# Flamingo gated block: halves of the exponentials added on GpSimd ahead of the ones product

## What is computed

```python
def _mha(query, key, value, Wq, bq, Wk, bk, Wv, bv, Wo, bo):
    q, k, v = ...                      # projections, split into 16 heads of 32
    scores = jnp.einsum('bhqd,bhkd->bhqk', q, k) / jnp.sqrt(jnp.asarray(dk, q.dtype))
    p = jax.nn.softmax(scores, axis=-1)
    x = jnp.einsum('bhqk,bhkd->bhqd', p, v)
    return jnp.einsum('bsd,ed->bse', x.transpose(0, 2, 1, 3).reshape(B, S, D), Wo) + bo
...
x = x + jnp.tanh(g_xattn[0]) * mha(layernorm(x), ctx, ctx, ...)
x = x + jnp.tanh(g_ffn[0]) * ffn(layernorm(x), ...)
```

## Time and profile before

| | before |
|---|---|
| median of 3 runs | 1910.21 us (1909.71 to 1914.14) |
| the profiled execution | 1910.74 us, span 1909.0 us |
| granted TensorE clock, mean | 0.97 of 2.4 GHz |
| TensorE busy | 1687.6 us, 88% |
| VectorE busy | 1441.6 us, 76% |
| ScalarE busy | 866.3 us, 45% |
| GpSimd busy | 497.3 us, 26% |
| attention phase | up to about 1350 us |
| ones product, busy | 135.7 us, 2048 records |
| product with v, busy | 138.1 us, 2048 records |

### The profile page before, as it was taken

The page is one execution under the profiler, slowest core; times in us unless marked ns, Lnnn a source line. Parts: engine busy times, 40 slices in busy tenths (PEclk is TensorE's granted clock), DMA queues, the critical chain, the costliest instruction groups (busy, mean ns, idle before and its releaser), DMA issues.

```text
span 1909.0 us, 36308 instructions
## 1 busy us (share of the span) xinstructions
PE 1687.6 (88%) x12892; PEld 832.0 (44%) x12892; DVE 1441.6 (76%) x1917; ACT 866.3 (45%) x1036; POOL 497.3 (26%) x686
## 2 busy tenths in 40 slices
PE   3788999989999899998999989986599999989787
PEld 3354444544445444454444444433344444434333
DVE  6648788787786877868778687777877778878555
ACT  2243433434335343353443533414777777756242
POOL 6123323223232232322323223212000000006634
PEclk6999999999999999999999999999799999999899
DMA  5233332323323233233332332225235454115897
GB/s 187 67 109 92 88 105 73 110 87 88 109 81 101 87 86 112 84 94 105 84 100 85 91 107 61 78 56 199 94 121 210 165 203 150 45 45 213 337 419 296
DMA packets 132189, 239.73 MB, mean 126 GB/s; under 512 B 17456, under 2 KB 66608, under 8 KB 129584
## 3 DMA queue, kind: packets, MB, share of 16 engines
q1 hardware_dynamic: 132144, 239.14, 38.1%
HBM read 126.10 MB, written 62.39 MB: 99 GB/s over the span
## 4 chain that ended last, share of the span: by engine, by line
issue 38%; PE 31%; DVE 16%; POOL 8%; DMA 5%; ACT 2%; POOLq 0%; DVEq 0%; SPq 0%; ACTq 0%
PE bank L1244 11%; PE bank L1149 5%; PE bank L1151 5%; PE bank L1150 5%; PE spair L1226 4%; DMA x<-out_dram 4%; DVE mx L842 3%; POOL xl L485 3%; DVE rs L834 3%; POOL yh L559 3%; DVE xbuf L806 2%; DVE v L826 1%; ACT xh L580 1%; DVE ndev L866 1%; DVE parts L821 1%
## 5 line engine op out<-in xcount | busy, mean ns | idle before, releaser
L593 ACT ACTIVATE pr<-spair 128x1024 f32<-128x1024 f32 x256 | 259.2, 1020 | 142.1 <-PE spair L1226 142.1
L842 DVE TENSOR_REDUCE mx<-spair 128x4 f32<-128x1024 f32 x256 | 304.4, 1212 | 0.0
L834 DVE RECIPROCAL rs<-bank 128x256 f32<-128x256 f32 x128 | 224.6, 1755 | 56.5 <-PE bank L1244 56.1
L821 DVE SCALAR_TENSOR_TENSOR parts<-bank,bqk,parts 128x512 f16<-128x512 f32 x128 | 94.5, 747 | 132.5 <-ACT parts L586 132.5
L515 POOL TENSOR_TENSOR ol<-o,oh 128x256 f16<-128x256 f32 x128 | 86.5, 675 | 389.7 <-ACT oh L602 380.8
L586 ACT ACTIVATE parts<-bank,bqk 128x512 f16<-128x512 f32 x128 | 88.0, 687 | 219.9 <-PE bank L1151 219.9
L1355 PE MATMUL spair<-xqT,wgT 128*128 128x512 bf16 x704 | 181.9, 381 | 1.2 <-ACT xqT L703 1.2
L1355 PE MATMUL spair<-xqT,wuT 128*128 128x512 bf16 x704 | 181.7, 381 | 0.0
L1244 PE MATMUL bank<-pr,v 128*32 128x256 f32 x2048 | 138.1, 387 | 27.2 <-DVE o L836 27.2
L1226 PE MATMUL spair<-stacks 128*128 128x256 f16 x1024 | 152.5, 275 | 6.5 <-DMA stacks<-mT 6.2
L686 ACT ACTIVATE sil<-spair,gsc 128x512 f32<-128x512 f32 x176 | 118.2, 680 | 74.9 <-PE spair L1355 74.9
(11 more groups left out here) (172 smaller groups left out, 3408.8 us busy)
## 6 DMA issues: line engine op xcount, KB each, us to landing
stacks<-parts SPq DMA_DIRECT2D x768, 64.0 KB, 2.0
x<-out_dram SPq DMA_DIRECT2D x32, 1024.0 KB, 11.0
h_spill<-hb SPq DMA_DIRECT2D x10, 2816.0 KB, 9.2
hb<-h_spill SPq DMA_DIRECT2D x10, 2816.0 KB, 15.6
xbuf<-in_x_dram SPq DMA_DIRECT2D x16, 1024.0 KB, 5.3
cbuf<-in_ctx_dram SPq DMA_DIRECT2D x16, 1024.0 KB, 5.3
xres<-in_x_dram SPq DMA_DIRECT2D x16, 1024.0 KB, 5.2
out_dram<-xres SPq DMA_DIRECT2D x16, 1024.0 KB, 4.3
```

The source lines that it names most:

```text
L593: act.activation(pr[:, u % 4, :, :, :].rearrange("p a b q -> p (a b q)"), spair[u % 2][:, :, :].rearrange("p a q -> p (a q)"), ACT.Exp, sc ...
L821: dve.scalar_tensor_tensor(out=parts[:, c, 2 * w + 1, :], in0=pj[g % 3][:, :], scalar=bqk[:, w, c:c + 1], in1=parts[:, c, 2 * w, :], op0=A ...
L834: dve.reciprocal(rs[:, g % 2, :], obank[:, S:2 * S]).then_inc(recip_done, 1)
L842: dve.tensor_reduce(mx[:, h:h + 2, b, :], spair[u % 2][:, :, :].rearrange("p a (q k) -> p a q k", q=KH), AX_X, ALU.max).then_inc(max_done, 1)
```

## The change

The two key halves of each unit's exponentials are added on GpSimd (`add_halves`, 128 partitions x 512 f32 elements) into a new tensor `ph` with four places, and the ones product runs over `ph` alone: four matmuls per group instead of eight. It comes behind the whole v product and waits for the sums of both units. GpSimd's queue is laid out anew: per group g first adds 2g and 2g + 1, then the low half of group g - 2, then in groups 0 to 3 one tile of the residual and in groups 4 to 6 one Newton step; the last two low halves stand behind the loop. `o32` has four buffers instead of two, and `norm` waits for the high and low halves of group g - 4.

```diff
-        o32 = alloc(p1, "o32", [P, 2, S], F32)
...
+        ph = alloc(p1, "ph", [P, 4, 2, S], F32)
+        o32 = alloc(p1, "o32", [P, 4, S], F32)
...
-            def root(n, which):
+            def root_step(n, which, step):
...
+                if step == 0:
+                    wait(pool, guessed[which], n + 1)
+                else:
+                    wait(pool, newton[which], k + 4 * step)
...
-            def residual(j):
+            def add_halves(j, u):
+
+                wait(pool, exp_done, j * NU + u + 1)
+                wait(pool, pv_mm, j * NGR + u // 2 - 1 + 2)
+                pool.tensor_tensor(ph[:, u % 4, :, :], pr[:, u % 4, :, 0, :], pr[:, u % 4, :, 1, :],
+                                   ALU.add).then_inc(halves_added, 1)
+
+            def residual(j, t):
 
                 wait(pool, res_in, j * 16 + 16)
-                for t in range(NT):
-                    pool.tensor_tensor(xres[:, t, :], xres[:, t, :], tgbo[:, :], ALU.add).then_inc(res_bias, 1)
+                pool.tensor_tensor(xres[:, t, :], xres[:, t, :], tgbo[:, :], ALU.add).then_inc(res_bias, 1)
...
             def body(j, nxt):
-                residual(j)
                 for g in range(NGR):
-                    o_low(j, g)
-                    if g == 3 and nxt is not None:
-                        x_rstds(nxt)
+                    add_halves(j, 2 * g)
+                    add_halves(j, 2 * g + 1)
+                    if g >= 2:
+                        o_low(j, g - 2)
+                    if g < NT:
+                        residual(j, g)
+                    elif g < NT + NEWTON and nxt is not None:
+                        root_step(nxt, 0, g - NT)
+                o_low(j, NGR - 2)
+                o_low(j, NGR - 1)
                 if nxt is not None:
                     low_parts(nxt)
                 x1_rstds(j)
...
             def norm(j, g):
                 wait(dve, pv_mm, j * NGR + g + 1 + 2)
-                if g >= 2:
-                    wait(dve, o_hi, j * NGR + g - 1)
-                    wait(dve, o_lo, j * NGR + g - 1)
+                if g >= 4:
+                    wait(dve, o_hi, j * NGR + g - 3)
+                    wait(dve, o_lo, j * NGR + g - 3)
...
-                for ones in (False, True):
-                    for kh in range(KH):
-                        for a in range(HPC):
-                            h = HPC * c + a
-                            at = S if ones else 0
-                            last = pe.matmul(obank[DK * a:DK * a + DK, at:at + S],
-                                             onesP[:, :] if ones else v[:, 2 * b + kh, DK * h:DK * h + DK],
-                                             pr[:, (2 * g + a // 2) % 4, a % 2, kh, :],
-                                             start=(kh == 0), stop=(kh == KH - 1))
+                for kh in range(KH):
+                    for a in range(HPC):
+                        h = HPC * c + a
+                        pe.matmul(obank[DK * a:DK * a + DK, 0:S], v[:, 2 * b + kh, DK * h:DK * h + DK],
+                                  pr[:, (2 * g + a // 2) % 4, a % 2, kh, :], start=(kh == 0), stop=(kh == KH - 1))
+                wait(pe, halves_added, j * NU + 2 * g + 2)
+                for a in range(HPC):
+                    last = pe.matmul(obank[DK * a:DK * a + DK, S:2 * S], onesP[:, :],
+                                     ph[:, (2 * g + a // 2) % 4, a % 2, :], start=True, stop=True)
                 last.then_inc(pv_mm, 1)
```

More of the change, by code:

```diff
@@ L187, in gated_block_kernel @@
         exp_done = sem("exp_done")
+        halves_added = sem("halves_added")
         pv_mm = sem("pv_mm")
@@ L491, in root @@
                 r0 = rt[:, which, :]
-                wait(pool, guessed[which], n + 1)
                 k = n * (4 * NEWTON - 1)
-                for step in range(NEWTON):
[L495 to L505, removed]
+                if step == 0:
+                    wait(pool, guessed[which], n + 1)
+                else:
+                    wait(pool, newton[which], k + 4 * step)
+                pool.tensor_tensor(a[0], r0, r0, ALU.mult).then_inc(newton[which], 1)
+                wait(pool, newton[which], k + 4 * step + 1)
+                pool.tensor_tensor(a[1], a[0], ve[:, which, :], ALU.mult).then_inc(newton[which], 1)
+                wait(pool, newton[which], k + 4 * step + 2, alone=True)
+                pool.tensor_scalar(a[2], a[1], -0.5, 1.5, ALU.mult, ALU.add).then_inc(newton[which], 1)
+                wait(pool, newton[which], k + 4 * step + 3)
+                if step < NEWTON - 1:
+                    pool.tensor_tensor(r0, r0, a[2], ALU.mult).then_inc(newton[which], 1)
+                else:
+                    pool.tensor_tensor(dst[:, :], r0, a[2], ALU.mult).then_inc(done, 1)
+            def root(n, which):
+                for step in range(NEWTON):
+                    root_step(n, which, step)
             def x_rstds(n):
@@ L514, in o_low @@
                 wait(pool, v_mm, j * NT + NT)
-                pool.tensor_tensor(ol[:, c, b * S:b * S + S], o32[:, g % 2, :], oh[:, c, b * S:b * S + S],
+                pool.tensor_tensor(ol[:, c, b * S:b * S + S], o32[:, g % 4, :], oh[:, c, b * S:b * S + S],
                                    ALU.subtract).then_inc(o_lo, 1)
-            def residual(j):
+            def add_halves(j, u):
[4 more added lines that the diff above has]
+            def residual(j, t):
                 wait(pool, res_in, j * 16 + 16)
-                for t in range(NT):
-                    pool.tensor_tensor(xres[:, t, :], xres[:, t, :], tgbo[:, :], ALU.add).then_inc(res_bias, 1)
+                pool.tensor_tensor(xres[:, t, :], xres[:, t, :], tgbo[:, :], ALU.add).then_inc(res_bias, 1)
             def x1_rstds(j):
@@ L601, in o_high @@
                 wait(act, v_mm, j * NT + NT)
-                act.activation(oh[:, c, b * S:b * S + S], o32[:, g % 2, :], ACT.Copy).then_inc(o_hi, 1)
+                act.activation(oh[:, c, b * S:b * S + S], o32[:, g % 4, :], ACT.Copy).then_inc(o_hi, 1)
             def turn_copies(n, ks):
@@ L830, in norm @@
                 wait(dve, pv_mm, j * NGR + g + 1 + 2)
-                if g >= 2:
-                    wait(dve, o_hi, j * NGR + g - 1)
-                    wait(dve, o_lo, j * NGR + g - 1)
+                if g >= 4:
+                    wait(dve, o_hi, j * NGR + g - 3)
+                    wait(dve, o_lo, j * NGR + g - 3)
                 dve.reciprocal(rs[:, g % 2, :], obank[:, S:2 * S]).then_inc(recip_done, 1)
                 wait(dve, recip_done, j * NGR + g + 1)
-                dve.tensor_tensor(o32[:, g % 2, :], obank[:, 0:S], rs[:, g % 2, :], ALU.mult).then_inc(norm_done, 1)
+                dve.tensor_tensor(o32[:, g % 4, :], obank[:, 0:S], rs[:, g % 2, :], ALU.mult).then_inc(norm_done, 1)
             def key_max(i, u):
```

## The result

The changed kernel takes 1964.08 us (median of 4 runs, 1961.82 to 1966.43) against 1911.76 of the kernel before in the same comparison: 1.0278 times as long, 95% interval 1.0265 to 1.0291. The profiled execution has a span of 1961.8 us, 52.9 above the 1909.0 of before.

A forecast was written before the change was run, and what follows sets the result against it. TensorE bounds pairs 2 to 6, VectorE the body's head and tail. Inner body 4.14 - 2.15 + 0.5 + 0.2 = +2.7 us, thirteen +35; with other bodies +39 on 1910.7 gives 1950, range 1915 to 1968.

The forecast's parts named there:

- rival (c): GpSimd's adds are dearer, 1.4 us each rather than 1.24: +13, 1963 us; chance 0.13.
- turns with ndev: At a body's head, adds 0 and 1 alternate with VectorE's four ndev spread instructions: +1.9 us.
- root stall: Pair 5's ones product waits 0.5 us because a root step stands ahead of adds 10 and 11 on GpSimd.
- new waits, met: TensorE's added wait between v and ones of each pair, already satisfied: 0.2 us a body (0 to 0.75).
- part 1: Pairs 1 to 6 each drop 8 of 16 ones records, 0.43 us: at most 2.6 us a body, 36 over 14.
- Parts 2 and 3: GpSimd adds take 1.24 us each; adds 2 and 3 wait behind xres's load, delaying pair 1's next score 2.24 us.
- Part 4: At a body's head, adds 0 and 1 take turns with VectorE's ndev spread: +1.9 us, pair 1's next score +4.14.
- rival (a): VectorE keeps its turn through the four ndev instructions, so only the load's wait holds: +11, 1921 us; chance 0.22.
- Part 5: Root steps in pairs 4 to 6: the first, awaiting VectorE's guess, delays adds 10 and 11; pair 5 stalls 0.5 us.
- Part 6: New wait between v and ones costs 0.2 us a body (0 to 0.75); four o32 buffers and later low halves 0.
- The other bodies: Outside the thirteen inner bodies: first -2.5 us, fourteenth +2.2 (no root), last +4.5 (2 to 5).

The follow-up runs named there:

- experiment 4: Changed kernel with residual tile t moved to group t + 1, so adds 2 and 3 stand ahead of the xres load wait: 1938.65 us, ratio 1.015.
- experiment 7: Changed kernel, pair 0's ones from both halves (no adds 0/1), residual tiles one group later; root steps in groups 5-7: 1884.74 us, in groups 4-6: 1880.62 us.
- experiment 6: Changed kernel with unread filler matmuls in pair 1, ten ahead of v and eight ahead of ones, all waits kept: 1939.5 us, ratio 1.0146.
- experiment 3: Changed kernel with adds made but TensorE's 16 ones records as before and not waiting for the sums; only later exponentials wait: 1954.73 us, ratio 1.0229.
- experiment 5: Changed kernel with pair 0's ones product from both key halves again and adds 0 and 1 gone: 1926.84 us, ratio 1.0098.

## Why the prediction was right, and where it was short

Forecast was 1950 with 1915 to 1968 and a slower kernel; it took 1964. The sign and the places were right, the size fell short: +52 measured, +39 forecast. The number alone would also fit rival (c), dearer adds, at 1963; but two adds start 1.23 us apart, not 1.4, so it isn't (c). Point by point for an inner body (mean over 13):

| step | forecast, us | measured, us |
|---|---|---|
| v of pair 1 later, turns with ndev | +1.9 | +1.92 |
| ones of pair 1 waits longer for its sums | +2.67 | +2.44 |
| from ones of pair 1 to v of pair 2 | -0.43 | +1.57 |
| v of pair 2 to v of pair 5 | -1.29 | -1.29 |
| v of pair 5 to v of pair 6, root stall in it | +0.1 | -0.06 |
| pair 6 to the next body | -0.43 | -0.56 |
| new waits, met | +0.2 | 0 |
| sum | +2.7 | +4.0 |

- What bounds the kernel: right. Halving the ones product alone gave 2.72 us a body against the 2.6 of part 1; the 0.12 more lie behind pair 6, where part 1 took all that pair 7 gains as swallowed.
- Parts 2 and 3: right. An add's median is 1.27 us, 1.23 from start to start; the load let GpSimd start 9.2 us behind the root (526.23 less 517.04; 9.5 was forecast), and moving the residual removed the wait. Where it was removed, however, the next wait took its place, as experiment 4 shows.
- Part 4: right, the turns rather than rival (a). The spread took 3.83 us where 3.8 was named, and it grows by 0.96 with each add beside it (0, 2 and 3 adds). The rule of the Trainium skill (SBUF — State Buffer, Who interferes with whom), that the first to issue keeps the port pair for its whole instruction, agrees again with these 3.83 us, though VectorE's instructions overlap, and with the 0.62 and 1.19 us of four elements in experiment 7.
- Part 5: right in kind, 0.35 us instead of 0.5: ones of pair 5 starts 1.24 us after v where it is due after 0.89. The first root step began 1.13 us after pair 4 (548.81 less 547.68), as worked out.
- Part 6: too dear. Ones follows v after 0.89 us with the wait met, as before it.
- What was missing: the third row of the table. The working took TensorE's work behind a wait at its usual duration. It waits 2.48 and 1.8 us within one pair, and the granted clock drops to half behind the first of them or, in other bodies, during the second. The term, put at nothing, is 2.0 us a body, 27 for the fourteen; experiment 6 took it away by itself and brought 24.6, net of what its fillers cost. The waits' lengths follow from the working (0.56 + 1.9 ahead of v, 2.7 behind it), and I didn't ask what they do to the clock. The trace of before could have warned me. In its last body v waits in pairs 1 to 7, and there TensorE ran a product at half clock (1.93 us for 1.07) behind such waits:

```profile
1310.19 1.07 PE L1244 MATMUL bank<-pr,v 128*32 128x256 f32 x16 [3.29 <-DVE o L836]
...
1315.28 1.93 PE L1244 MATMUL bank<-pr,v 128*32 128x256 f32 x16 [2.17 <-DVE o L836]
```

- On the clock the Trainium skill (TensorE: Matmul & The Clock Gate, Part 1) says that the gate halves the array's clock when TensorE has been idle and that activity lifts it again; experiments 3 and 6 agree, with 82.4 against 80.72 us for the same instructions and 80.6 for a body kept busy.
- The other bodies: the first gained 2.8 us against 2.5 forecast (its period 75.42 for 78.20). The fourteenth lost 2.6 against 2.2 (76.32 for 73.71). The last was taken at 4.5 and came to about 2 (from its first v to the end of its ndev spread 72.8 us for 70.8), so that this error and the missing clock partly cancelled, by luck. The first v itself started 1.8 us earlier, with a granted clock of 0.97 in the opening where it was 0.81; experiments whose code there is the same show 0.81 to 0.97, so this isn't the change. With the 52.1 of the thirteen these add up to 52 of the 52.9 us.

Not settled: why a wait of 2.25 or 2.46 us brings the half clock in some bodies and not in others. Its length alone doesn't decide: in experiment 4 three bodies kept the full clock behind 3.48 us. Which bodies are spared repeats in fours in experiments 3 and 4, in experiment 5 it doesn't; no run here was made to tell what decides. On average over 13 bodies the half clock cost 1.1 us with the wait of 2.46 ahead of v alone (experiment 3), 1.0 with the wait ahead of ones alone (experiment 5), and 2.0 with both.

## What to carry to other kernels

Before moving elementwise work to an idle engine, go down that engine's queue and ask of each wait in it who is now behind it, and which VectorE instruction from SBUF to SBUF runs at that moment: here 42 us were to be gained, and three bad neighbours turned them into 52 lost. Price a new wait on TensorE twice, as idle time and as slower work behind it. A pair whose end isn't on the path can keep the longer way; leaving it out of the offload cost nothing and removed the worst neighbour.

## What the runs showed of the hardware that I had not expected

- Behind short waits TensorE's clock can fall to half. Two idle stretches in one pair, 2.5 and 1.1 to 2.4 us, did it in each inner body of the changed kernel (granted clock 0.61 and 0.64 for the next 9.3 us in the one shown); one of 2.46 did it in nine of 13, one of 3.48 in ten. Eighteen matmuls that nobody reads, put into the idle time, made the kernel 24.6 us faster.
- VectorE and GpSimd take turns even when VectorE's instructions overlap, at 0.96 us for each add of 1.27, and even for a VectorE instruction of four elements per partition: 0.62 and 1.19 us instead of 0.17.
- A TensorE wait that is already met, between two products on the same bank, costs nothing that shows: 0.89 us from v to ones with and without it.
